# A recurrent-attention and mixture-of-experts layer: adaptation matmuls by sequence in column and row groups, router logits in four column groups turned by VectorE

## The chip, the core and the metric

The kernel runs on one core of one Trainium2 chip. The metric is the device time of one execution in microseconds; the time before is the median of three runs.

## The reference

32 sequences of 256 tokens with 128 channels, all in float32. The layer is a recurrent attention followed by a feed-forward layer with 16 experts, each with a residual and a layer norm:

```python
delta = shifted - h
x_lerp = h + delta * x_proj_mu
x0 = tanh(x_lerp @ xl_w1.T) @ xl_w2.T + xl_b2        # rank 32, then 5 * 32
x1 = tanh(x0).reshape(B, T, 5, 32)
mus = einsum('btnr,hnr->btnh', x1, x_out_w) + x_bias  # 5 mixing vectors per token
r, k, v, g, w = projections of (h + delta * mu_i)
o = scan over the tokens of S * w + k v, read with r, plus a bonus term
x = layernorm(h + (groupnorm(o) * gn_w + gn_b) * silu(g) @ o_w.T)
logits = x @ router_w + expert_bias                   # 16 experts
top 2 of the logits, softmax over the two
out = layernorm(x + shared_ffn(x) + weighted sum of the two experts' ffn(x))
```

The change touches the lines of `x0` and `x1` (called the adaptation here) and of `logits`.

## The kernel before

The work is in two stages. In the first, the 32 sequences are taken in 16 units of two sequences (512 tokens). In the second, the tokens, sorted by expert into DRAM, are taken in tiles of 256 rows through the experts; at the end the results are gathered and normed.

In the first stage each engine has a body written out by hand, with an offset for every step: `at(1, a_adapt0)` does step `a_adapt0` of unit i+1 in iteration i. So one iteration interleaves four units: the a-steps (mixing and projections) of one, the b-steps (attention in chunks of 32 tokens, in five levels) of the next older, the c-steps (norm, residual, router) of the one before that, and the f-steps (shared expert) of the oldest. Every engine runs its list in order; semaphores tie the lists together. A step waits with `done` for its inputs and with `before` for the last reader of what it overwrites.

TensorE's order in an iteration is: a_v, b_o, f_up 0, a_turn, c_place, level 0, f_up 1, a_adapt0, level 1, a_adapt1, f_up 2, level 2, mix w and r, f_up 3, decay_hid, level 3, w, r, c_attn, mix k and v, level 4, f_down, mix g, k, k_tok, c_turn, b_kv, c_logits, g. The steps that the change and the prediction touch:

- `a_adapt0` (TensorE, L331) multiplies the weights `xl_w1`, stored twice side by side (64 columns), with `x_lerp` of both sequences (512 columns) into bank P1, partitions 0 to 63. ScalarE's `a_adapt0` (L610) takes Tanh of it.
- `a_adapt1` (L337, L338) makes the 160 outputs in two matmuls of 32 rows: 128 outputs from partitions 0 to 31 into P0 and 32 outputs from partitions 32 to 63 into P1. ScalarE's `a_adapt1a` (L616) and `a_adapt1b` (L622) take Tanh with bias.
- `by_seq` (L309) is the form that the projections already have: one matmul per sequence, 64 outputs each, on output partitions 0 to 63 and 64 to 127. `mix` (L318) multiplies 32 rows of adapt1 by 128 outputs; mixes w and r, and k and v, stand in pairs, in different row groups and banks.
- `c_turn` (L466) transposes x; ScalarE copies it to x1T (L744). `c_logits` (TensorE, L472) uses each of the four 128-token tiles of x1T as weights and `router_w` (16 columns) as the moving side, so that the logits come out with tokens on partitions. VectorE's `c_logits` (L1089) adds the bias.
- VectorE's order behind that is: b_state (the scan, L1016), f_base (L1181), a_gate (L992), c_top (max, index, top_gap at L1103, chosen, either, seen up to L1114). TensorE's `c_place` (L478) waits for `seen`.
- ScalarE's order there is: x1T, b_kv (kv_sb, L704, which the scan waits for), a_k (L665, which TensorE's a_v waits for), k_near, gate, v, b_o.
- GpSimd's order is: rstd, step 4, chunk_decay, mixed V and G, scatter 0 (two indirect writes, L900, which wait for VectorE's slots), step 0 (L866, L868, L870), scatter 1, o_rstd, step 1, scatter 2, step 2, scatter 3, step 3. `b_step` i gives what level i+1 reads.

A float32 matmul shows as two records in the trace, each with its own weight load.

Of the kernel before, what the change touches and what calls it, by code (L numbers as in the profile page):

```python
# [17 lines left out]
UB = 2  # L18
# [22 lines left out]
COLS = (["x_mu", "xl_b2a", "xl_b2b"] + [f"x_bias{n}" for n in range(NMIX)] + ["w_b", "bonus", "gn_w", "gn_b", "tile_no", "tile_row", "par0", "par1"]  # L41
# [4 lines left out]
MATS = {"xl_w1": (C, 2 * RANK), "xl_w2": (2 * RANK, RANK * NMIX), "x_out_a": (128, C), "x_out_b": (RANK, C),  # L46
        "r_w": (C, HK), "k_w": (C, HK), "w_w1": (C, GATE), "w_w2": (UB * GATE, HK), "v_w": (C, HV), "g_w": (C, HV),
        "ident": (128, 128), "near": (128, L), "token_no": (128, TILES * TOPK),
        "o_w": (HV, C), "before": (128, 128), "ones": (128, 128), "router_w": (C, EXPERTS), "expert_bias": (128, EXPERTS),
# [9 lines left out]
def build(nc, hidden, mats_dram, cols_dram, masks_dram, w1_dram, w2_dram, b2_dram, out):  # L59
# [8 lines left out]
    with ctx:  # L68
# [34 lines left out]
        adapt0 = sb("adapt0", [2 * RANK, UT])  # L103
# [41 lines left out]
        logits = sb("logits", [128, TILES, EXPERTS])  # L145
# [48 lines left out]
        psP = [pb(f"psP{i}", [128, 512]) for i in range(2)]  # L194
# [4 lines left out]
        P0, P1 = psP[0][:, :], psP[1][:, :]  # L199
# [102 lines left out]
        def _(pe):  # L302
# [25 lines left out]
            def a_adapt0(u):  # L328
                before(pe, "gate", u)
                done(pe, "x_lerp", u)  # L330
                mm(P1[0:2 * RANK, :], mat("xl_w1"), flat(x_lerp), start=True, stop=True).then_inc(sem("adapt0_ps"))  # L331

            def a_adapt1(u):
                done(pe, "hT", u)
                done(pe, "adapt0", u)
                pe.nop(nofuse=True)
                mm(P0, mat("xl_w2")[0:RANK, 0:128], adapt0[0:RANK, :], start=True, stop=True)  # L337
                mm(P1[0:RANK, :], mat("xl_w2")[RANK:2 * RANK, 128:160], adapt0[RANK:2 * RANK, :], start=True, stop=True).then_inc(sem("adapt1_ps"))  # L338
# [130 lines left out]
            def c_logits(u):  # L469
                done(pe, "x1T", u)  # L470
                for j in range(TILES):
                    last = mm(O0[:, j * EXPERTS:(j + 1) * EXPERTS], x1T[u % 2][:, j * 128:(j + 1) * 128], mat("router_w"), start=True, stop=True)  # L472
                last.then_inc(sem("logits_ps"))
# [120 lines left out]
        def _(act):  # L594
# [11 lines left out]
            def a_adapt0(u):  # L606
# [3 lines left out]
                A(adapt0[:, :], P1[0:2 * RANK, :], ACT.Tanh).then_inc(sem("adapt0"))  # L610

            def a_adapt1a(u):
# [3 lines left out]
                A(adapt1a[:, :], P0, ACT.Tanh, bias=col("xl_b2a")).then_inc(sem("adapt1a"))  # L616

            def a_adapt1b(u):
# [3 lines left out]
                A(adapt1b[:, :], P1[0:RANK, :], ACT.Tanh, bias=col("xl_b2b", RANK)).then_inc(sem("adapt1b"))  # L622
# [133 lines left out]
            def body(at):  # L756
# [3 lines left out]
                at(-2, b_kv)  # L760
                at(-1, a_k)
# [190 lines left out]
        def _(dve):  # L952
# [131 lines left out]
            def c_logits(u):  # L1084
                if u == 0:
                    dve.wait_ge(sem("late_weights"), 16)
                done(dve, "logits_ps", u)
                dve.nop(nofuse=True)
                V.tensor_tensor(logits[:, :, :], O0[:, 0:TILES * EXPERTS].rearrange("p (n e) -> p n e", e=EXPERTS),  # L1089
                                mat("expert_bias").unsqueeze(1).broadcast_to([128, TILES, EXPERTS]), ALU.add).then_inc(sem("logits"))  # L1090

            def c_top(u):
# [3 lines left out]
                for j in range(TILES):  # L1096
                    last = V.max(top_val[:, j, :], logits[:, j, :])
# [3 lines left out]
                for j in range(TILES):  # L1101
                    last = V.max_index(top_idx[:, j, :], top_val[:, j, :], logits[:, j, :])
# [179 lines left out]
def pack(i):  # L1282
# [9 lines left out]
    put("xl_w2", np.tile(g("xl_w2").T, (2, 1)))  # L1292
# [11 lines left out]
    put("router_w", f("router_w"))  # L1304
    put("expert_bias", np.broadcast_to(f("expert_bias"), (128, EXPERTS)))
# [14 lines left out]
    for n in range(NMIX):  # L1320
        putc(f"x_bias{n}", g("x_bias")[n])
    putc("w_b", np.tile(g("w_b"), UB))
# [27 lines left out]
```

## Time and profile before

| | us |
|---|---|
| median of three runs (1012.99 to 1021.11) | 1017.16 |
| the profiled execution | 1020.37 |
| its span, first to last instruction | 1018.5 |
| TensorE (PE) busy | 847.5 (83%) |
| GpSimd (POOL) busy | 575.9 (57%) |
| VectorE (DVE) busy | 518.1 (51%) |
| ScalarE (ACT) busy | 488.0 (48%) |

The span has a start of some 110 us in which the pipeline fills, 13 like units up to about 555 us, a drain up to 660 us, the experts up to 950 us and the last norm. The mean granted TensorE clock is 0.921 of full speed (2.4 GHz); half of full speed is the other level, 1.2 GHz.

How to read it: PE is TensorE's matmuls and PEld its weight loads, which overlap them. Matmuls are pipelined, so the time of a record is longer than the distance to the next one; what a group costs is read from the distance between the starts of two groups, or from the chain that ended last, which counts each piece once. "x4" is the number of records in a group. The bracket behind a row says how long the engine was idle before it and who released it. Where two instructions of one engine overlap by a tenth of a microsecond, the second started before the first had written its last result.

### The profile page before, as it was taken

The numbers are of one execution on the slowest core, as the hardware profiler recorded it, in microseconds if no ns is written. First come the engines' busy times: TensorE is split into PE (matmuls) and PEld (weight loads), VectorE is DVE, ScalarE is ACT, GpSimd is POOL, SyncE is SP. The second block draws the span as 40 slices with busy tenths as digits, with TensorE's granted clock in tenths as the row PEclk, the third lists the DMA queues.
The fourth block names the chain that finished last, engine by engine and source line by source line (L and its number), as shares of the span: only waits on it lengthen the run. The fifth ranks groups of instructions, "written<-read, shape, count | busy, mean of one in ns | idle before, by whom it ended". The sixth has DMA issues, their size and how long they took to land.

```text
span 1018.5 us, 31274 instructions
## 1 busy us (share of the span) xinstructions
PE 847.5 (83%) x11556; PEld 597.0 (59%) x11557; DVE 518.1 (51%) x1478; ACT 488.0 (48%) x1121; POOL 575.9 (57%) x707
## 2 busy tenths in 40 slices
PE   4687999999989999999898856899999999999000
PEld 1233565456545554555455544799999999989000
DVE  2234576667676766676677443233333333322465
ACT  1233554555455545554555331466556666555244
POOL 2232556676667666766676747255555554555465
PEclk9976799999999999999999785899999999999655
DMA  4000111011101110111011331322222222221573
GB/s 136 21 2 6 34 50 49 27 51 55 49 25 55 52 52 24 53 54 52 24 50 33 96 103 51 100 74 64 74 66 71 62 62 71 59 61 36 164 224 107
DMA packets 74493, 63.67 MB, mean 63 GB/s; under 512 B 8178, under 2 KB 65912, under 8 KB 74256
## 3 DMA queue, kind: packets, MB, share of 16 engines
q1 hardware_dynamic: 56720, 40.86, 14.4%
q0 software_dynamic: 9216, 17.07, 5.1%
q10 hardware_dynamic: 8448, 4.20, 1.4%
q8 instruction: 79, 1.29, 0.5%
q14 instruction: 30, 0.25, 0.1%
HBM read 38.55 MB, written 25.63 MB: 63 GB/s over the span
## 4 chain that ended last, share of the span: by engine, by line
PE 69%; DVE 11%; issue 7%; ACT 5%; POOL 3%; DMA 2%; another core or an unknown queue 0%; DVEq 0%; SPq 0%; ACTq 0%; POOLq 0%
PE psO L573 14%; PE psB L562 13%; PE psB L408 7%; PE psO L507 6%; PE psP L318 6%; PE psO L501 4%; PE psP L309 3%; PE psP L337 2%; DVE top_gap L1103 2%; PE psB L427 2%; PE psP L331 2%; PE psP L553 2%; PE psP L338 2%; PE psO L460 2%; DVE mixed L983 1%
## 5 line engine op out<-in xcount | busy, mean ns | idle before, releaser
L934 POOL DMA_INDIRECT expert_results<-yw_all,rows x160 | 157.2, 983 | 158.4 <-ACT yw_all L799 129.5
L900 POOL DMA_INDIRECT dispatched_rows<-rows,slot x128 | 138.5, 1082 | 59.3 <-issue 29.3
L573 PEld LDWEIGHTS psO<-w_sb,hide 128*128 128x128 f32 x1280 | 154.8, 192 | 7.2 <-issue 3.5
L573 PE MATMUL psO<-w_sb,hide 128*128 x1280 | 156.5, 275 | 1.3 <-ACT hide L791 1.3
L791 ACT ACTIVATE hide<-psB,w_ring 128x256 f32<-128x256 f32 x320 | 125.1, 474 | 60.1 <-PE psB L562 56.5
L562 PE MATMUL psB<-x1T,w_ring 128*128 128x256 f32 x640 | 153.1, 382 | 0.3 <-DVE x1T L1224 0.2
L562 PEld LDWEIGHTS psB<-x1T,w_ring 128*128 128x128 f32 x640 | 116.3, 192 | 14.1 <-issue 1.2
L1237 DVE TENSOR_TENSOR kv_sb<-psO,b_sb 128x256 f32<-128x256 f32 x80 | 34.0, 425 | 176.7 <-PE psO L573 139.6
L799 ACT ACTIVATE yw_all<-kv_sb,rows 128x128 f32<-128x128 f32 x160 | 55.5, 394 | 81.4 <-issue 47.6
L983 DVE SCALAR_TENSOR_TENSOR mixed<-psP,cols,delta 128x512 f32<-128x512 f32 x80 | 58.0, 742 | 60.0 <-PE psP L309 31.6
L408 PEld LDWEIGHTS psB<-w_ring 32*32 32x32 f32 x4096 | 49.4, 108 | 65.8 <-issue 62.7
L501 PE MATMUL psO<-x1T,mats 128*128 128x512 f32 x128 | 78.4, 697 | 7.2 <-ACT w_sb L754 6.2
L1009 DVE COPY_PREDICATED pair<-masks,psB 128x512 f32<-128x512 uint32 x64 | 46.5, 726 | 60.8 <-PE psB L408 60.5
L408 PE MATMUL psB<-w_ring 32*32 32x64 f32 x4096 | 68.8, 239 | 9.3 <-issue 6.8
L754 ACT ACTIVATE w_sb<-psO,cols 128x512 f32<-128x512 f32 x64 | 43.3, 677 | 55.5 <-PE psO L501 49.2
L507 PE MATMUL psO<-mats,w_sb 128*128 128x128 f32 x512 | 65.1, 288 | 0.9 <-ACT w_sb L754 0.9
L507 PEld LDWEIGHTS psO<-mats,w_sb 128*128 128x128 f32 x512 | 62.1, 202 | 3.8 <-ACT w_sb L754 2.4
L885 POOL TENSOR_TENSOR o_rstd<-o_var,minus_half 128x16 f32<-128x16 f32 x16 | 50.9, 3182 | 19.0 <-DVE o_var L1027 16.2
L853 POOL TENSOR_TENSOR mixed<-mixed,hT 128x512 f32<-128x512 f32 x32 | 34.7, 1085 | 40.2 <-DVE mixed L983 40.2
L866 POOL TENSOR_TENSOR tot<-tot 128x64 f32<-128x64 f32 (+1 forms) x64 | 17.2, 269 | 70.6 <-PE psB L408 37.3
L733 ACT ACTIVATE rows<-z,z_shift,z_rstd 128x128 f32<-128x128 f32 x64 | 26.4, 482 | 59.8 <-DVE z_shift L1068 52.2
L1231 DVE COPY w_ring<-w_sb 128x516 f32 x80 | 34.4, 431 | 35.3 <-issue 35.3
(164 smaller groups left out, 1455.1 us busy)
## 6 DMA issues: line engine op xcount, KB each, us to landing
rows<-dispatched_rows SPq DMA_DIRECT2D x80, 132.0 KB
w_sb<-expert_results SPq DMA_DIRECT2D x16, 512.0 KB, 3.9
h_tok<-in_hidden SPq DMA_DIRECT2D x16, 256.0 KB, 4.7
h_res<-in_hidden SPq DMA_DIRECT2D x16, 256.0 KB, 3.2
out<-mixed ACTq DMA_DIRECT2D x16, 256.0 KB, 2.5
w_sb<-in_w SPq DMA_DIRECT2D x14, 256.0 KB, 4.8
expert_results<-yw_all,rows POOLq DMA_INDIRECT x160
dispatched_rows<-pad_rows SPq DMA_DIRECT2D x17, 132.0 KB, 3.7
```

The lines of the kernel that those rows point to most:

```text
L318: mm(ps, w, a, start=True, stop=True, **kw).then_inc(sem(f"mix_ps{n}"))
L408: last = mm(psL[32 * c4:32 * c4 + 32, g, c2 * 2 * L:(c2 + 1) * 2 * L].rearrange("p (a t) -> p a t", t=L), Ks[p, t], Rs[p, :, t], start=Tru ...
L501: mm(O1, mat("shared_w1")[:, c * 128:(c + 1) * 128], x1T[u % 2][:, :], start=True, stop=True).then_inc(sem(f"hid_ps{c}"))
L507: last = mm(O1[:, j * 128:(j + 1) * 128], hid[:, c, j * 128:(j + 1) * 128], mat("shared_w2")[:, c * 128:(c + 1) * 128], start=(c == 0), st ...
L562: last = mm(up_ps(p)[:, c // 2, (c % 2) * ST:(c % 2 + 1) * ST], w1b[i % W_RING][:, c * 128:(c + 1) * 128], xTe[p], start=True, stop=True)
L573: last = mm(psO[:, p, s * 128:(s + 1) * 128], hide[p][:, c, s * 128:(s + 1) * 128], w2_sb[:, bass.ds(e, 1), c, :].rearrange("p e c -> p (e ...
L791: last = A(hide[p][:, c, :], psB[:, 2 * p + c // 2, (c % 2) * ST:(c % 2 + 1) * ST], ACT.Relu, bias=w1b[i % W_RING][:, HIDDEN + c:HIDDEN + ...
L799: last = A(yw[i][:, s, :], ye[p][:, s, :], ACT.Copy, scale=row_in[i][:, s, AT_W:AT_W + 1])
L885: G.tensor_tensor(o_rstd[:, :], o_var[:, :], minus_half[:, :], ALU.pow).then_inc(sem("o_rstd"))
L900: G.indirect_dma_start(rows_dram[:, :], bass.IndirectOffsetOnAxis(slot[u % 2][:, j, k:k + 1], 0), rows[k][u % 2][:, j, :], None).then_inc( ...
L934: G.indirect_dma_start(back_dram[:, :], bass.IndirectOffsetOnAxis(row_in[i][:, s, AT_DEST:AT_DEST + 1].bitcast(u32), 0), yw[i][:, s, :], N ...
L983: V.scalar_tensor_tensor(mixed[MIX_BUF[n]][:, :, :], unflat((P0, P1)[MIX_BANK[n]]), col(f"x_bias{n}"), delta[:, :, :], ALU.add, ALU.mult). ...
```

## The change

The adaptation is done by sequence. `a_adapt0` uses `by_seq`: each sequence has its own 64 output partitions, and adapt0 becomes a tile of 128 partitions by 256 columns. `xl_w2` is stored four times, and `a_adapt1` has four matmuls of 256 columns: for the first 128 outputs of sequence 0 (rows 0 to 31) and sequence 1 (rows 64 to 95) into the first halves of P0 and P1, then for the last 32 outputs of both into the second halves. The two Tanh evictions read from both banks.

The router's weights are padded to 32 columns and become the stationary side; the tokens are the moving side, in four column groups. Column group q takes the q-th block of 32 tokens of each of the four tiles, 128 columns. The logits then have experts on partitions; ScalarE adds the bias while it copies them out of PSUM (a new step between b_kv and a_k), and VectorE transposes them in blocks of 32x32, which gives tokens on partitions again. VectorE no longer reads PSUM for them. The top-2 steps read the first 16 of 32 columns.

```diff
 MATS:
-"xl_w2": (2 * RANK, RANK * NMIX)
+"xl_w2": (UB * 2 * RANK, RANK * NMIX)
-"router_w": (C, EXPERTS), "expert_bias": (128, EXPERTS),
+"router_w": (C, L),
...
-        adapt0 = sb("adapt0", [2 * RANK, UT])
+        adapt0 = sb("adapt0", [UB * 2 * RANK, T])
...
-        logits = sb("logits", [128, TILES, EXPERTS])
+        logits_T = sb("logits_T", [128, TILES * L])
+        logits = sb("logits", [128, TILES, L])
...
-        psP = [pb(f"psP{i}", [128, 512]) for i in range(2)]
+        psP_both = pb("psP", [128, 2, 512])
+        psP = [psP_both[:, i, :] for i in range(2)]
...
             def a_adapt0(u):
                 before(pe, "gate", u)
                 done(pe, "x_lerp", u)
-                mm(P1[0:2 * RANK, :], mat("xl_w1"), flat(x_lerp), start=True, stop=True).then_inc(sem("adapt0_ps"))
+                by_seq(P1, mat("xl_w1"), x_lerp).then_inc(sem("adapt0_ps"))
...
-                mm(P0, mat("xl_w2")[0:RANK, 0:128], adapt0[0:RANK, :], start=True, stop=True)
-                mm(P1[0:RANK, :], mat("xl_w2")[RANK:2 * RANK, 128:160], adapt0[RANK:2 * RANK, :], start=True, stop=True).then_inc(sem("adapt1_ps"))
+                for b in range(UB):
+                    p = slice(64 * b, 64 * b + RANK)
+                    mm(psP[b][:, 0:T], mat("xl_w2")[p, 0:128], adapt0[p, :], start=True, stop=True)
+                for b in range(UB):
+                    p = slice(64 * b, 64 * b + RANK)
+                    last = mm(psP[b][0:RANK, T:2 * T], mat("xl_w2")[p, 128:160], adapt0[p, :], start=True, stop=True)
+                last.then_inc(sem("adapt1_ps"))
...
             def c_logits(u):
                 done(pe, "x1T", u)
-                for j in range(TILES):
-                    last = mm(O0[:, j * EXPERTS:(j + 1) * EXPERTS], x1T[u % 2][:, j * 128:(j + 1) * 128], mat("router_w"), start=True, stop=True)
+                pe.nop(nofuse=True)
+                x = x1T[u % 2][:, :].rearrange("p (n q t) -> p q n t", q=4, t=L)
+                for q in range(4):
+                    last = mm(O0[32 * q:32 * q + 32, 0:TILES * L].rearrange("p (n t) -> p n t", t=L), mat("router_w"), x[:, q, :, :],
+                              start=True, stop=True, tile_position=(0, 32 * q))
                 last.then_inc(sem("logits_ps"))
...
-                A(adapt0[:, :], P1[0:2 * RANK, :], ACT.Tanh).then_inc(sem("adapt0"))
+                A(adapt0[:, :], P1[:, 0:T], ACT.Tanh).then_inc(sem("adapt0"))
...
-                A(adapt1a[:, :], P0, ACT.Tanh, bias=col("xl_b2a")).then_inc(sem("adapt1a"))
+                A(unflat(adapt1a[:, :]), psP_both[:, :, 0:T], ACT.Tanh, bias=col("xl_b2a")).then_inc(sem("adapt1a"))
...
-                A(adapt1b[:, :], P1[0:RANK, :], ACT.Tanh, bias=col("xl_b2b", RANK)).then_inc(sem("adapt1b"))
+                A(unflat(adapt1b[:, :]), psP_both[0:RANK, :, T:2 * T], ACT.Tanh, bias=col("xl_b2b", RANK)).then_inc(sem("adapt1b"))
...
+            def c_logits(u):
+                done(act, "logits_ps", u)
+                before(act, "logits", u)
+                act.nop(nofuse=True)
+                A(logits_T[:, :], O0[:, 0:TILES * L], ACT.Identity, bias=col("router_b")).then_inc(sem("logits_T"))
...
                 at(-2, b_kv)
+                at(-3, c_logits)
                 at(-1, a_k)
...
             def c_logits(u):
-                if u == 0:
-                    dve.wait_ge(sem("late_weights"), 16)
-                done(dve, "logits_ps", u)
-                dve.nop(nofuse=True)
-                V.tensor_tensor(logits[:, :, :], O0[:, 0:TILES * EXPERTS].rearrange("p (n e) -> p n e", e=EXPERTS),
-                                mat("expert_bias").unsqueeze(1).broadcast_to([128, TILES, EXPERTS]), ALU.add).then_inc(sem("logits"))
+                done(dve, "logits_T", u)
+                V.transpose(logits[:, :, :].rearrange("p n e -> p (n e)"), logits_T[:, :]).then_inc(sem("logits"))
```

## Rows read from the trace of the kernel before

**Rows 1.** Windows: us, then busy us (instructions) PE, PEld, DVE, ACT, POOL, clock, DMA.
```profile
50.00:108.00 58.00, 47.88 (x779) 22.19 (x778) 24.97 (x43) 18.79 (x40) 21.47 (x34) 0.72 0.06 18
...
190.00:194.00 4.00, 4.00 (x69) 1.41 (x68) 0.93 (x4) 2.12 (x4) 2.81 (x4) 0.67 0.12 36
...
280.00:314.00 34.00, 31.19 (x593) 18.31 (x593) 23.66 (x66) 17.44 (x38) 23.22 (x29) 1.00 0.16 46
```

**Rows 2.** Chain that ended last, in order of time, 289 to 305: start, us.
```profile
289.83 1.00 PE psP L331 x2
...
291.64 1.09 PE psP L337 x2
...
292.74 0.97 PE psP L338 x2
...
294.76 0.62 PE psB L408 x36
...
301.91 0.58 PE psP L309 x4
...
303.58 1.10 PE psP L318 x4
```

**Rows 3.** Timeline, 290 to 300: start, us, engine, line, out<-in, idle before.
```profile
290.95 0.59 ACT L610 ACTIVATE adapt<-psP 64x512 f32<-64x512 f32 x1 [2.71 <-PE psP L331]
...
292.59 0.73 POOL L870 TENSOR_TENSOR w_ring<-w_ring,tot 128x256 f32<-128x256 f32 x1
...
298.17 1.01 POOL L900 DMA_INDIRECT dispatched_rows<-rows,slot  x1 [0.15 <-POOL w_ring L870]
...
298.60 0.69 DVE L988 TENSOR_TENSOR mixed<-mixed,hT 128x512 f32<-128x512 f32 x1
```

**Rows 4.** Timeline of PE in the first unit.
```profile
10.75 1.97 PE L331 MATMUL psP<-x_lerp,mats 128*64 128x512 f32 x2 [3.81 <-DVE x_lerp L972]
13.51 2.04 PE L337 MATMUL psP<-adapt,mats 32*128 32x512 f32 x2 [0.79 <-issue]
15.48 1.91 PE L338 MATMUL psP<-adapt,mats 32*32 32x512 f32 x2
...
22.61 1.12 PE L309 MATMUL psP<-mixed,mats 128*64 128x256 f32 x4 [1.70 <-DVE mixed L988]
```

**Rows 5.** Lines L628, L653, L1040: duration ns min/median/max.
```profile
L628 ACT ACTIVATE decay_hid<-psP x16: 383/383/384, 23.8 to 539.9; 128x256 f32<-128x256 f32 x16
...
L653 ACT ACTIVATE exp_w<-psP,cols x16: 473/473/475, 25.6 to 541.7; 128x256 f32<-128x256 f32 x16
...
L1040 DVE STREAM_TRANSPOSE w_sb<-w_sb x16: 683/691/711, 85.0 to 597.5; 128x512 f32<-128x512 f32 x16
```

**Rows 6.** Timeline, 312 to 322.
```profile
312.89 1.06 PE L472 MATMUL psO<-mats,x1T 128*128 128x16 f32 x8
...
313.52 0.68 ACT L704 ACTIVATE kv_sb<-psB 128x256 f32<-128x256 f32 x1
...
313.98 0.43 ACT L665 ACTIVATE w_ring<-psP 128x256 f32<-128x256 f32 x1
314.06 0.22 DVE L1089 TENSOR_TENSOR logits<-psO,mats 128x64 f32<-128x64 f32 x1 [0.23 <-PE psO L472]
314.32 1.22 DVE L1016 TENSOR_TENSOR_SCAN state<-chunk_decay,kv_sb 128x512 f32<-128x512 f32 x1
...
314.66 1.80 POOL L900 DMA_INDIRECT dispatched_rows<-rows,slot  x1 [1.76 <-DVE dest L1173]
...
317.74 1.71 DVE L1103 TENSOR_TENSOR top_gap<-top_val 128x4 f32<-128x4 f32 x1
...
318.58 0.84 POOL L870 TENSOR_TENSOR w_ring<-w_ring 128x256 f32<-128x256 f32 x1
...
321.16 0.43 PE L478 MATMUL psO<-either,mats 128*128 128x64 f32 x2 [0.63 <-DVE seen L1114]
```

**Rows 7.** Timeline, one scatter of a late unit.
```profile
582.51 1.10 POOL L900 DMA_INDIRECT dispatched_rows<-rows,slot  x1 [1.80 <-DVE dest L1173]
```

More of the change, by code:

```diff
@@ L39 @@
 MIX_BUF = {n: i % 2 for i, n in enumerate(MIX_ORDER)}
-COLS = (["x_mu", "xl_b2a", "xl_b2b"] + [f"x_bias{n}" for n in range(NMIX)] + ["w_b", "bonus", "gn_w", "gn_b", "tile_no", "tile_row", "par0", "par1"]
+COLS = (["x_mu", "router_b", "xl_b2a", "xl_b2b"] + [f"x_bias{n}" for n in range(NMIX)] + ["w_b", "bonus", "gn_w", "gn_b", "tile_no", "tile_row", "par0", "par1"]
         + [f"shared_b1_{c}" for c in range(HC)])
 COL = {n: i for i, n in enumerate(COLS)}
-MATS = {"xl_w1": (C, 2 * RANK), "xl_w2": (2 * RANK, RANK * NMIX), "x_out_a": (128, C), "x_out_b": (RANK, C),
+MATS = {"xl_w1": (C, 2 * RANK), "xl_w2": (UB * 2 * RANK, RANK * NMIX), "x_out_a": (128, C), "x_out_b": (RANK, C),
         "r_w": (C, HK), "k_w": (C, HK), "w_w1": (C, GATE), "w_w2": (UB * GATE, HK), "v_w": (C, HV), "g_w": (C, HV),
         "ident": (128, 128), "near": (128, L), "token_no": (128, TILES * TOPK),
-        "o_w": (HV, C), "before": (128, 128), "ones": (128, 128), "router_w": (C, EXPERTS), "expert_bias": (128, EXPERTS),
+        "o_w": (HV, C), "before": (128, 128), "ones": (128, 128), "router_w": (C, L),
         "expert_no": (128, EXPERTS), "region": (128, EXPERTS),
@@ L198, in build @@
         O0, O1 = psO[:, 0, :], psO[:, 1, :]
-        P0, P1 = psP[0][:, :], psP[1][:, :]
+        P0, P1 = psP
         flat = lambda t: t.rearrange("p a b -> p (a b)")
@@ L1096, in c_top @@
                 for j in range(TILES):
-                    last = V.max(top_val[:, j, :], logits[:, j, :])
+                    last = V.max(top_val[:, j, :], logits[:, j, 0:EXPERTS])
                 last.then_inc(sem("top_steps"))
@@ L1101, in c_top @@
                 for j in range(TILES):
-                    last = V.max_index(top_idx[:, j, :], top_val[:, j, :], logits[:, j, :])
+                    last = V.max_index(top_idx[:, j, :], top_val[:, j, :], logits[:, j, 0:EXPERTS])
                 V.tensor_tensor(top_gap[:, :], top_val[:, :, 1], top_val[:, :, 0], ALU.subtract).then_inc(sem("top_gap"))
@@ L1291, in pack @@
     put("xl_w1", np.tile(g("xl_w1").T, (1, 2)))
-    put("xl_w2", np.tile(g("xl_w2").T, (2, 1)))
+    put("xl_w2", np.tile(g("xl_w2").T, (UB * 2, 1)))
     put("x_out_a", g("x_out_w").T[:128])
@@ L1303, in pack @@
     put("ones", np.ones((128, 128), np.float32))
-    put("router_w", f("router_w"))
-    put("expert_bias", np.broadcast_to(f("expert_bias"), (128, EXPERTS)))
+    put("router_w", np.pad(f("router_w"), ((0, 0), (0, L - EXPERTS))))
     put("expert_no", np.broadcast_to(np.arange(EXPERTS, dtype=np.float32), (128, EXPERTS)))
@@ L1321, in pack @@
         putc(f"x_bias{n}", g("x_bias")[n])
+    putc("router_b", np.tile(np.pad(f("expert_bias"), (0, L - EXPERTS)), 4))
     putc("w_b", np.tile(g("w_b"), UB))
```

## The prediction

> **What bounds the kernel now.** I read the windows by stage first, then the chain that ended last in order of time, then the timeline of one unit. Of the 16 units (two sequences each) 13 run alike, with a new one begun every 34 us. In such a unit TensorE is busy 31.19 of 34 us at a granted clock of 1.00, which is 2.4 GHz [rows 1]. The chain shows that this is real: from the place matmuls (L478) to the KV matmuls it stays almost wholly on TensorE, and the three adaptation matmuls L331, L337 and L338 lie on it with 1.00, 1.10 (291.64 to 292.74) and 0.97 us [rows 2]. The rest of the unit is not TensorE's: from the eviction of kv_sb (ACT, L704) the chain goes to the scan (DVE, L1016), through VectorE's top-2 work to `seen`, and back to TensorE, which sat idle 0.63 us before L478 [rows 6]. So time off the adaptation counts in full, time off the logits matmuls counts only if the scan starts earlier, and anything put ahead of the scan costs.
>
> **adapt0.** One 128x64 matmul over 512 columns becomes two over 256 columns, on output partitions 0-63 and 64-127: exactly what `by_seq` (L309) does, four records in 0.58 us. Saved: 1.00 - 0.58 = 0.42 us. Tanh then reads 128x256 instead of 64x512: 0.59 us [rows 3] becomes 0.38 (L628, same form) [rows 5]. That matters only for whether adapt1 waits: the new adapt0 ends near 290.41, Tanh runs 290.53 to 290.91 (0.12 us for the hop, as from TensorE's end at 290.83 to Tanh at 290.95), and level 1 frees TensorE 0.42 us before 291.64, at 291.2. It doesn't wait, by about 0.2 us.
>
> **adapt1.** Before, L337 (32x128) and L338 (32x32) ran one after the other, 2.07 us together. After, there are two pairs of 256 columns; in each pair the two matmuls use row groups 0 and 64 and different banks. The nearest rows are L318, where two 32x128 matmuls over 512 columns in different row groups and banks take 1.10 us as a pair, and L309 with 0.58 for a pair of 256 columns [rows 2]. I take 0.63 for the first pair (128 weight columns) and 0.58 for the second: saved 2.07 - 1.21 = 0.86 us. Both ends: 2.07 - 2 x 0.55 (half of L318) = 0.97, and, should the pairs run singly, 2.07 - 4 x 0.58 = -0.25. I stay near L318, which is the same shape. The two Tanh that follow read as many columns as before, now from two banks: no cost.
>
> In a steady unit this is 1.28 us off the chain. What could take it back is what level 2 waits for: it starts at 294.76 and would start at 293.5; its latest input from GpSimd, L870, ends at 293.32 [rows 2, 3], and that itself follows level 1, so 0.2 us or more are left. Everything behind it to L427 is released by TensorE's own results and moves along. 13 x 1.28 = 16.6 us.
>
> The first unit runs at 1.2 GHz: L331 1.97 us, L337 and L338 together 3.88 (13.51 to 17.39), and the `by_seq` form 1.12 [rows 4]. Saved there: 0.85 + (3.88 - 2.24) + 0.21 of Tanh = 2.7 us. The second and third unit are partly at the low clock as well (0.72 on the mean from 50 to 108 us) [rows 1], but level 1 covers the Tanh and level 2 part of adapt1; I take 2.3 each. Together 7.3 us.
>
> **Router logits on TensorE.** Eight records with 128-column weight loads (0.91 us from L472 at 312.89 to the next matmul) become eight with 32-column loads in four column groups. Whatever they take up to 0.91 us, the result is there by about 314.0, and ScalarE is on kv_sb until then. What TensorE gains here is hidden: g follows earlier, but `a_v` waits for k_done. I cost it at nothing. If that cover went, it would be worth at most 0.6 us a unit.
>
> **Router logits on ScalarE and VectorE.** ScalarE gets one instruction more, a 128x128 eviction with bias from PSUM, between kv_sb and the copy of K (L665). From L610 and L628 a column costs 0.81 ns, so 128 columns take 0.28 us; the bias adds 0.09 (L653 against L628) [rows 3, 5]. It starts where L665 does now, 313.98, and ends at 314.35. VectorE's transposition can start 0.12 us later (the hop from kv_sb's end at 314.20 to the scan at 314.32), at 314.47. It replaces the addition L1089, and **the scan is behind it in VectorE's queue**. For its length, 512 columns took 0.69 (L1040) and so did the addition L988; with 0.22 for the 64 columns of L1089 that is 1.05 ns a column, so 0.29 us. Bounds: 0.17 (a quarter of L1040) and 0.35 (a half); for ScalarE 0.28 and 0.47. The scan starts at about 314.75 instead of 314.32 [rows 6]: 0.43 us late, between 0.23 and 0.6.
>
> Behind ScalarE's new wait stand the copy of K, k_near, the gate and v. K comes 0.3 us later and `a_v` waits for it, but `b_o`, the next on TensorE, waits for the scan's end, which is later still. Behind the scan stand base_out, the gate, the top-2 and `seen`, and TensorE waits for `seen`. Does GpSimd swallow it? top_gap (L1103), a 128x4 subtraction, took 1.71 us and ended with GpSimd's L870 at 319.4, so there is a stall that could absorb 0.43 us. But GpSimd's steps hang on the scan themselves: the scatter L900 began at 314.66, inside the scan, and ended 0.92 us after the scan's end (315.54) [rows 6]; free it takes 1.10 [rows 7]. So it asks for something that the scan holds 0.18 us after its start, at 314.84, and the scan will hold it from 314.75. Scatters, L866 to L870 and top_gap then move along with the scan, and the whole 0.43 us is paid: 13 x 0.43 = 5.6 us.
>
> A rule speaks for a higher price. The Trainium skill ("SBUF — State Buffer", section "SBUF: two separate sides") says that VectorE with two SBUF inputs and a GpSimd operation lock each other out, and that the one that starts first holds the port for its whole instruction. Top_gap against L870 agrees with it. Taken at its word, the scatter at 314.66 would now be first and hold the scan; see the third rival for what that gives.
>
> **Sum.** -16.6 - 7.3 + 5.6 = -18.3 us. The profiled execution took 1020.37 (span 1018.5), 3.2 more than the median; from it I would get 1002.1, from the median of 1017.16 it is 998.9. Forecast: 999.
>
> **Rivals.**
> 1. *The scatter gets ahead of the scan.* If the two hops cost 0.1 us more than I think, the scan starts behind 314.84, and the scatter ends at 315.8 instead of 316.46. GpSimd's steps end 0.7 us earlier, near 318.7, and top_gap with them. Then TensorE is the later one: 321.16 - 0.63 + 0.43 = 320.96, so L478 starts 0.20 us earlier than now, not 0.43 later [rows 6]. 13 x 0.63 = 8.2 us more: 991. My estimate misses this by only 0.1 us. Chance 0.17.
> 2. *The clock falls more often.* After the narrow matmuls of one unit the granted clock was 0.67 over 4 us, so 1.2 GHz for about 2.6 us of them [rows 1]. Shorter bursts with the same waits may bring that into every unit. Much of it falls in waits for VectorE; at 0.4 us a unit it costs 5 us: 1004. Chance 0.10.
> 3. *The scan is held by the scatter* until 315.76 and starts at 315.8: 1.5 us late, 13 x 1.5 = 19.5 instead of 5.6: 1013. Against it: L988, with two SBUF inputs, began 0.43 us into a scatter and took its ordinary 0.69 us [rows 3]. Chance 0.08.
> 4. *Row groups 0 and 64 don't overlap*, so the change doesn't do in adapt1 what it says: 13 x (0.42 - 0.25) = 2.2, early units some 1.5, less 5.6: 1019. L318 speaks against it. Chance 0.10.
> 5. *Slower: neither row nor column groups overlap in these places*, for instance because other tile shapes stand between them. adapt0 then costs 2 x 0.58 - 1.00 = 0.16 more and adapt1 0.25 more, 13 x 0.41 + 1.5 early = 6.8, plus 5.6: 1030. It turns to slower once the adaptation gains less than 0.43 us a unit. L309 and L318 both speak against it. Chance 0.04.
>
> **How the numbers follow.** Forecast 0.48 (its own range 994 to 1004), rivals 0.17, 0.10, 0.08, 0.10, 0.04, and 0.03 for something slower that I don't see. The range 987 to 1014 holds the forecast and the first three rivals, with some 4 us left for the spread of the runs at the lower end; above it are rivals 4 and 5 and the rest, 0.17. About 1% (10 us) is what a measurement of this kernel can tell from no change. Faster by over 1% (below 1007): 0.48 + 0.17 + 0.10 = 0.75. Within 1%: rivals 3 and 4, 0.18. Slower: rival 5 and the rest, 0.07.
>
> **What would show it.** Each step has its place in the profile after: adapt0 as four records in 0.6 us and adapt1 as eight in 1.2; level 2 about 1.3 us closer behind L478; the ScalarE eviction 0.37 and the transposition 0.29 us, with the scan right behind it; the first scatter still some 1.7 us long and top_gap some 1.7 (rival 1: scatter 1.1, top_gap 0.6 or less); the period 33.2 us instead of 34. The prediction is wrong if level 2 waits for GpSimd, if adapt1 shows four starts 0.5 us apart, or if the scan starts much more than 0.5 us after kv_sb.

## The result and the profile after

The change made the kernel slower: 1028.27 us (median of 6, 1023.91 to 1029.31) against 1017.7 for the kernel before beside it (6 runs), a ratio of 1.0082 with a 95% interval of 1.0053 to 1.0111. The forecast was 999, with a range of 987 to 1014. The profiled execution took 1023.91, its span was 1022.1 us and its mean clock 0.913. It was the shortest of the six, so the two profiles, spans of 1022.1 and 1018.5 us, show only 3.6 of the 10.6 us between the medians. Ratios and intervals are made from fast runs alone; of the runs below, three of the four of the kernel with the bad place (1068.87 to 1072.02, over 1.5% above its fastest, 1050.65) count as slow, and it has no ratio.

On the page of the profile after, PE is busy 16 us less than before (831.1 against 847.5). But the small matmuls of the levels, with the same count as before, now have 15.6 us of idle time behind which the profile shows no releaser ("issue"); before it was 6.8:

```profile
PE 831.1 (81%) x11652; PEld 589.7 (58%) x11653; DVE 517.9 (51%) x1478; ACT 487.4 (48%) x1137; POOL 579.0 (57%) x707
...
L415 PE MATMUL psB<-w_ring 32*32 32x64 f32 x4096 | 73.3, 243 | 16.8 <-issue 15.6
```

The same line of the page before:

```profile
L408 PE MATMUL psB<-w_ring 32*32 32x64 f32 x4096 | 68.8, 239 | 9.3 <-issue 6.8
```

The third scan starts at 132.64 instead of 143.53, so the early units gained 10.9 us; the forecast had 7.3. Behind the last steady scan they take 464.5 and 464.1 us. All of the loss lies in the 12 units between. Windows over them, first of before, then of after (us; busy us of PE, PEld, DVE, ACT, POOL; clock):

```profile
143.53:553.98 410.45, 377.42 (x7105) 221.69 (x7104) 284.20 (x793) 210.45 (x432) 278.52 (x348) 0.99 0.15 44
```
```profile
132.64:558.01 425.37, 372.86 (x7176) 219.90 (x7175) 284.19 (x793) 209.39 (x444) 282.85 (x349) 0.96 0.15 43
```

They grew by 14.9 us where the forecast had them shrink by 10. Each operation that the change touches is nevertheless nearly as short as forecast. adapt1 takes from 290.80 to 292.03, 1.23 us (forecast 1.21, before 2.07 [rows 2]), in the timeline of after:

```profile
290.80 0.75 PE L341 MATMUL psP<-adapt,mats 32*128 32x256 f32 x4
291.48 0.62 PE L344 MATMUL psP<-adapt,mats 32*32 32x256 f32 x4
292.03 1.12 PE L511 MATMUL psO<-x1T,mats 128*128 128x512 f32 x2
```

And the router's new way, in the same view, which answers to [rows 6]:

```profile
311.70 0.43 PE L481 MATMUL psO<-x1T,mats 128*32 128x128 f32 x8
...
312.06 1.13 PE L396 MATMUL psP<-mixed,mats 128*128 128x512 f32 x2
...
312.94 0.34 ACT L760 ACTIVATE logits_T<-psO,cols 128x128 f32<-128x128 f32 x1
...
313.31 0.31 DVE L1103 STREAM_TRANSPOSE logits<-logits_T 128x128 f32<-128x128 f32 x1 [0.52 <-ACT logits_T L760]
313.54 1.18 DVE L1033 TENSOR_TENSOR_SCAN state<-chunk_decay,kv_sb 128x512 f32<-128x512 f32 x1
313.62 2.01 POOL L917 DMA_INDIRECT dispatched_rows<-rows,slot  x1 [1.77 <-DVE dest L1186]
```

The logits matmuls take 0.36 us instead of 0.91, the eviction 0.34 (forecast 0.37), the transposition 0.31 (0.29), and the scatter still ends 0.9 us after the scan, as forecast.

One undisturbed unit, scan to scan, shows the failure in small: first of before, then of after.

```profile
348.46:382.54 34.08, 31.29 (x594) 18.39 (x592) 23.69 (x67) 17.53 (x37) 23.19 (x29) 1.00 0.16 45
```
```profile
347.78:381.88 34.10, 29.98 (x598) 18.09 (x598) 23.82 (x67) 17.50 (x38) 23.73 (x29) 1.00 0.16 46
```

TensorE is busy 1.31 us less, and the unit is as long as it was. The timeline of PE and POOL shows where it went. Before, level 2 (L408) was:

```profile
293.50 1.06 POOL L900 DMA_INDIRECT dispatched_rows<-rows,slot  x1 [0.17 <-POOL w_ring L870]
...
294.69 1.12 PE L408 MATMUL psB<-w_ring 32*32 32x64 f32 x50
294.86 0.96 POOL L900 DMA_INDIRECT dispatched_rows<-rows,slot  x1 [0.30 <-issue]
296.22 0.41 PE L408 MATMUL psB<-w_ring 32*32 32x64 f32 x14 [0.40 <-issue]
```

After (L415):

```profile
360.89 1.06 POOL L917 DMA_INDIRECT dispatched_rows<-rows,slot  x1 [0.17 <-POOL w_ring L887]
360.89 0.84 PE L415 MATMUL psB<-w_ring 32*32 32x64 f32 x45
362.15 0.32 PE L415 MATMUL psB<-w_ring 32*32 32x64 f32 x6 [0.42 <-issue]
362.25 0.96 POOL L917 DMA_INDIRECT dispatched_rows<-rows,slot  x1 [0.30 <-issue]
362.88 0.32 PE L415 MATMUL psB<-w_ring 32*32 32x64 f32 x5 [0.41 <-issue]
363.59 0.36 PE L415 MATMUL psB<-w_ring 32*32 32x64 f32 x8 [0.39 <-issue]
363.88 1.13 PE L320 MATMUL psP<-adapt1a,mats 32*128 32x512 f32 x4
```

Level 2 starts 1.3 us earlier against the scan, as forecast, and so comes to lie under both writes of scatter 2. After 45 records it proceeds by 5 to 8 records every 0.7 us, with gaps of 0.4, until the scatter has ended (363.21). Its last records start 0.38 us behind that end, and before they started 0.40 us behind it (296.22 against 295.82). The mix behind it (L320) starts 16.10 us after the scan, against 16.30 before. The gain is returned on the spot. In the kernel before, this wait already lay on the chain that ended last:

```profile
295.38 0.11 issue
295.50 0.32 PE psB L408 x5
295.82 0.40 issue
296.22 0.41 PE psB L408 x11
```

Six of the twelve units are 35.0 to 37.9 us long, and together they hold nearly the whole of the 14.9 us; the other six take 34.07 to 34.66. In five of the six long ones b_o (L454) stalls too; this is the unit from 275.99 (37.55 us):

```profile
278.33 0.82 PE L454 MATMUL psB<-state,w_ring 32*32 32x32 f32 x35
...
279.63 0.76 PE L454 MATMUL psB<-state,w_ring 32*32 32x32 f32 x51 [0.48 <-issue]
...
281.25 0.43 PE L454 MATMUL psB<-state,w_ring 32*32 32x32 f32 x26 [0.86 <-issue]
...
284.06 0.60 ACT L721 ACTIVATE o_sb<-psB 128x512 f32<-128x512 f32 x1 [4.33 <-remote]
...
284.91 0.61 PE L415 MATMUL psB<-R_near,K_near 32*32 32x64 f32 x39 [1.35 <-ACT o_sb L721]
```

The first gap, of 0.48 after 35 records, stands in every unit, before (0.46) as after. The second, 0.86 after 86, does not. In this unit ScalarE's copy of o also starts 2.4 us after b_o's end, and level 0 waits for it. That is dearer than the stall itself. In the units of this profile without a stall behind record 42 the copy starts 0.1 to 0.3 us after b_o's end; in the 18 profiles together it starts more than 0.5 us late only in units with such a stall, and then up to 2.8 us.

### The profile page after: what moved, and what is told of

Read it like the earlier page. It is cut to its first block, busy times and chain, and to the rows that moved or that the text cites. A ratio compares the mean times of both kernels' runs of the same rounds, so it can differ in the third digit from the quotient of the medians.

```text
span 1022.1 us, 31499 instructions
## 1 busy us (share of the span) xinstructions
PE 831.1 (81%) x11652; PEld 589.7 (58%) x11653; DVE 517.9 (51%) x1478; ACT 487.4 (48%) x1137; POOL 579.0 (57%) x707
## 3 DMA queue, kind: packets, MB, share of 16 engines
q8 instruction: 80, 1.31, 0.6%
## 4 chain that ended last, share of the span: by engine, by line
PE 70%; DVE 9%; issue 7%; ACT 6%; POOL 4%; another core or an unknown queue 2%; DMA 1%; ACTq 0%; DVEq 0%; SPq 0%; POOLq 0%
PE psO L583 14%; PE psB L572 14%; PE psB L415 7%; PE psP L320 6%; PE psO L511 5%; PE psO L517 5%; PE psP L311 4%; PE psB L434 2%; PE psO L467 2%; PE psP L563 2%; PE psB L454 1%; ACT mixed L836 1%; PE psP L341 1%; PE psP L367 1%
## 5 line engine op out<-in xcount | busy, mean ns | idle before, releaser
L511 PE MATMUL psO<-x1T,mats 128*128 128x512 f32 x128 | 87.0, 767 | 11.5 <-ACT w_sb L770 8.5
L415 PEld LDWEIGHTS psB<-w_ring 32*32 32x32 f32 x4096 | 51.7, 110 | 70.7 <-issue 67.9
L415 PE MATMUL psB<-w_ring 32*32 32x64 f32 x4096 | 73.3, 243 | 16.8 <-issue 15.6
L870 POOL TENSOR_TENSOR mixed<-mixed,hT 128x512 f32<-128x512 f32 x32 | 34.7, 1085 | 36.8 <-DVE mixed L1000 36.8
```

Of the source, the lines that this page charges most:

```text
L415: last = mm(psL[32 * c4:32 * c4 + 32, g, c2 * 2 * L:(c2 + 1) * 2 * L].rearrange("p (a t) -> p a t", t=L), Ks[p, t], Rs[p, :, t], start=Tru ...
L511: mm(O1, mat("shared_w1")[:, c * 128:(c + 1) * 128], x1T[u % 2][:, :], start=True, stop=True).then_inc(sem(f"hid_ps{c}"))
```

## The experiments

The theories were these. *Supply*: TensorE's instructions arrive too slowly where many short matmuls stand together, either because GpSimd's scatters run beside them or because of where the blocks lie in which they are fetched (the page shows 80 packets and 1.31 MB in an instruction queue, so 16 KB each; I took a block to be 256 instructions). *Logits*: the scan's delay is dearer than I thought. *Clock*: the changed rhythm lowers the clock. Each group of runs had its own runs of the kernel before, with which the ratios are made (medians 1005.02, 1022.85, 1019.48 and 1021.79 us).

### First group: the halves, a shift, the scatters moved

The adaptation alone (all of the diff's lines on adapt0, adapt1, psP and `xl_w2`):

> Only the adaptation by sequence; the logits as in the kernel before. Theory A (TensorE's instructions come late in level 2 whenever the adaptation is shorter): the 1.3 us saved per unit come back as idle time ended by issue in level 2, so the time is near the kernel before, 1008 to 1020 (the early units keep some 7 us). Rival B (the loss is the scan behind the new logits steps, 0.4 us a unit): without them the adaptation's gain shows in full, about 993.

978.11 us (977.53 to 986.29), ratio 0.9729 (0.9653 to 0.9805), with units of 31.9 to 32.9 us. The logits alone (the rest of the diff):

> Only the router logits in column groups with the transposition; the adaptation as before. Rival B: 13 units x 0.4 us later scan, about 1023, and no further idle time in level 2. Theory A: the same 0.4 us a unit on the scan, but one issue gap of 0.4 us in level 2 as before, and in b_o further issue gaps only where a block of instructions ends in it; 1020 to 1030.

1012.44 us, ratio 1.0046 (0.9998 to 1.0093): no gain, and perhaps a loss, with b_o stalls of 1.1 to 1.7 us in six units. Then the whole change with 60 instructions put in at the start of TensorE's stream:

```diff
             pe.wait_ge(sem("weights"), 32)
+            for _ in range(15):
+                mm(psP[0][0:32, 0:8], mat("ident")[0:32, 0:32], mat("ident")[0:32, 0:8], start=True, stop=True)
```

> The changed kernel with 15 small matmuls (60 instructions, under 1 us, before the first input is there) at TensorE's start, nothing else. Theory C (in some units b_o is held where TensorE's instruction stream passes the end of a block of 256): the units with a long gap in b_o move by one, since every unit moves the place by some 30 records and the shift moves it back by 30; time within 5 us of the changed kernel. Rival: the long gaps come from transfers of that moment (loads of h and weights, scatters), then they stay in the same units (third, sixth, seventh, eleventh, twelfth).

989.71 us, ratio 0.9822 (0.9758 to 0.9886): the time did not stay within 5 us of the changed kernel. The b_o stalls did move by one unit, as the place in the stream would have it: in after they stand in units 3, 7, 11 and 12, here in 4, 8, 12 and 13. And the whole change with two scatters behind the GpSimd steps that level 3 and 4 need:

```diff
-                at(-1, c_scatter, 2)
                 at(2, b_step, 2)
-                at(-1, c_scatter, 3)
+                at(-1, c_scatter, 2)
                 at(2, b_step, 3)
+                at(-1, c_scatter, 3)
```

> The changed kernel with GpSimd's scatters 2 and 3 behind its steps 2 and 3 instead of ahead of them, so that none is issued while TensorE is in level 2. Theory A, with the scatters as the cause of the late instructions: the three gaps of 0.4 us in level 2 go, level 3 may get some, 0.5 to 1.2 us a unit, 1012 to 1022. Rival (instructions come at a fixed rate whatever GpSimd does): the gaps in level 2 stay and the time is that of the changed kernel, 1028.

987.38 us, ratio 0.981 (0.9741 to 0.9878). Read alone, this says that the shift cured the kernel. The traces say something else: in all four the gaps in level 2 and the 0.46 us gap in b_o are missing in nearly every unit, in those without a shift as well; and with no gaps to cure, the moved scatters gained nothing over the shift. Level 2 of the adaptation alone ran beside the same scatter without a halt:

```profile
305.96 1.04 PE L414 MATMUL psB<-w_ring 32*32 32x64 f32 x64
305.99 1.06 POOL L906 DMA_INDIRECT dispatched_rows<-rows,slot  x1 [0.17 <-POOL w_ring L876]
306.93 1.13 PE L319 MATMUL psP<-adapt1a,mats 32*128 32x512 f32 x4
```

The kernel before was faster here as well (1005.02, against 1019 to 1023 in all later groups). So the unshifted kernels had to be run again.

### Second group: controls

> The changed kernel once more, nothing altered, as the control for the shifted one and the one with the scatters moved. If the place of TensorE's instruction stream decides (theory A), it is 0.5 to 1.1% slower than the kernel before again, with two kinds of stalls in its trace: three gaps of about 0.41 us within the 64 small matmuls of level 2 in every unit, and gaps of 0.7 to 1.4 us within b_o in some units. If the stalls belong to the chip or to where the program was loaded on it (theory B), it is 1.5 to 3% faster here, with a steady period of about 32.1 us and no gap in level 2, like its shifted copy.

1034.29 us, ratio 1.0095 (1.0069 to 1.0122): the loss is real, and the gaps are back.

> The kernel before once more, nothing altered, for its trace on this chip. Theory A (place of the stream): steady periods of 34.0 to 34.4 us again, with one gap of 0.40 us in level 2 after 50 matmuls. Theory B (chip or loading): no gap of 0.40 in level 2 and periods of about 33.6 us (34.08 less the 0.40); its time within 1% of its own earlier median on this chip.

1020.65 us, ratio 0.9976 (0.9949 to 1.0004): periods of 34.1 us and the gap of 0.42 in level 2 in every unit.

> The kernel before with 60 more instructions (15 tiny fp32 matmuls into a scratch bank) at the start of TensorE's stream, nothing else. Theory A: its time moves by 0.5 to 3% either way against the kernel before, and the gaps within b_o turn up in other units. Theory B: within 0.3% of the kernel before, since the sum of its stalls is the same wherever the blocks of instructions lie.

1026.82 us, ratio 1.0054 (1.0024 to 1.0084): small, but three b_o stalls instead of one in the units 2 to 15. It is 0.6% over the unchanged copy e6, at the low end of what the place of the blocks was expected to do.

> The changed kernel with 120 more instructions (30 tiny fp32 matmuls) at the start of TensorE's stream. Theory A: its time differs from the unshifted one of the same chip by over 1%, as the copy with 60 would have to. Theory B: within 0.3% of the unshifted one run beside it.

1037.42 us, ratio 1.0123 (1.0081 to 1.0166). That is 0.3% over the unshifted copy e5, not the 1% or more that was expected of the place of the blocks. The shift is no cure. What sets the first group apart isn't the kernel; nor is it the chip, since the last group below ran on the same one and has the gaps. That stays open.

The controls also price the clock. The unit from 355.43 of the unchanged copy has the same gaps as the unit of after shown above, at a clock of 0.91 instead of 1.00, and takes 1.9 us longer:

```profile
355.43:391.44 36.01, 32.71 (x598) 18.79 (x598) 23.66 (x67) 17.51 (x38) 23.84 (x29) 0.91 0.15 43
```

### Third group: the place of the blocks, the scatters again

```diff
             def c_place(u):
+                pad(O0, 14)
+                nc.tensor.transpose(O0[0:32, 300:332], mat("ident")[0:32, 0:32], mat("ident")[0:32, 0:32])
                 done(pe, "seen", u)
```

> The changed kernel with TensorE's instruction stream padded: tiny matmuls of 32x8 into a part of the bank that nothing reads, 23 before the first input and, in each unit, 14 and a turn of 32x32 ahead of the wait for seen, so that the stream advances by 1279 instructions a unit (5 times 256 less 1) instead of 1221. Theory A (b_o stalls where the stream passes instruction 194 modulo 256 and the block behind it is not there yet): this point now lies after 21 to 27 of b_o's 112 matmul records in every unit from the second on, where no profile has shown a stall; no gap over 0.3 us follows there in any unit (the one after 34 to 36 records, of 0.46 to 0.50 us, may stay), no unit of 37 us is left, and the kernel is 10 us or more faster than its twin with the bad place. Theory B (the stalls in b_o come from transfers or scatters that run beside it): some four to six units have them still, at other records, and the twins agree within 0.5%.

> The twin of the one before: the same 14 tiny matmuls and the turn in each unit, but none before the first input, so that instruction 194 modulo 256 lies after 66 to 73 of b_o's 112 records in every unit from the second on. Theory A: a gap of 0.4 to 1.7 us at just that record in 14 of 16 units, periods 1 to 3.5 us longer than with the good place, in sum 15 to 45 us slower than its twin. Theory B: within 0.5% of it.

1023.39 us (1017.56 to 1027.74) with the good place; 1050.65, 1068.87, 1070.01 and 1072.02 with the bad one. The two kernels differ by 92 instructions ahead of the first input. The comparison to rest on is with the one run of 1050.65: 27 us, and still 23 above the longest run with the good place. How much of the rest, up to 49 us, belongs to the place is not shown. The profile is of the run of 1072.02. b_o with the good place, then with the bad:

```profile
275.27 0.82 PE L462 MATMUL psB<-state,w_ring 32*32 32x32 f32 x35
...
276.56 1.00 PE L462 MATMUL psB<-state,w_ring 32*32 32x32 f32 x77 [0.47 <-issue]
```
```profile
289.87 0.82 PE L461 MATMUL psB<-state,w_ring 32*32 32x32 f32 x35
...
291.19 0.58 PE L461 MATMUL psB<-state,w_ring 32*32 32x32 f32 x34 [0.50 <-issue]
...
292.19 0.65 PE L461 MATMUL psB<-state,w_ring 32*32 32x32 f32 x43 [0.42 <-issue]
```

The stall behind records 67 to 73 stands in all units from 3 to 15 of the bad one, and in none of the units 2 to 15 of the good one. The units 4 to 14 take 38.2 to 40.5 us against 34.2 to 36.3. A stall of 0.4 us is the least of it: in the units 4 to 15 ScalarE's copy of o starts 2.4 to 2.8 us after b_o's end, with the good place 0.12; f_up (L520) waits up to 1.55 us for ScalarE; and the clock over the twelve units is 0.83 instead of 0.94:

```profile
134.24:554.73 420.49, 381.59 (x7524) 224.45 (x7523) 282.71 (x792) 209.61 (x444) 282.26 (x348) 0.94 0.15 43
```
```profile
132.33:601.27 468.94, 421.24 (x7524) 237.31 (x7523) 284.47 (x792) 209.47 (x444) 278.47 (x348) 0.83 0.13 39
```

But the good place doesn't win either: 1.003 (0.9998 to 1.0062). Its level 2 gaps are all there.

> Only the adaptation by sequence, with the logits as before, padded in the same way with the good place (records 21 to 34). If the logits' new form is what makes b_o's block come late (it did in 6 of 6 places between records 56 and 111, the adaptation alone in 3 of 7), this is as fast as or faster than the padded full change; against the kernel before it is 1.5 to 3.5% faster. If the adaptation's many short matmuls are the burden, it loses against the kernel before on a chip with gaps in level 2.

1018.77 us, ratio 0.997 (0.9946 to 0.9994): the lower end of what was expected is missed; the level 2 gaps eat this version's gain too.

> The changed kernel with the scatters of a tile behind the products of steps 2 and 3 on GpSimd rather than ahead of them, for its trace on this chip. If the scatters that run under level 2 hold TensorE's supply of instructions up (three gaps of about 0.41 us), the gaps go or move to level 3, where the scatters now run, and step 2 starts right behind the matmuls. If the gaps belong to level 2's own 64 matmuls, they stay.

998.55 us, ratio 0.9806 (0.9738 to 0.9873), in a group whose other kernels have the gaps. This is the cure. Between scan 3 and scan 15 no scatter touches level 2 any more. Level 2 runs through, and the mix starts 14.11 us after the scan instead of 16.10:

```profile
313.42 0.85 PE L415 MATMUL psB<-w_ring 32*32 32x64 f32 x64
314.21 1.13 PE L320 MATMUL psP<-adapt1a,mats 32*128 32x512 f32 x4
...
315.84 1.06 POOL L917 DMA_INDIRECT dispatched_rows<-rows,slot  x1 [0.18 <-POOL w_ring L887]
```

The scatter's first write now runs beside a matmul of 512 columns, which needs few instructions, and a wait; the second reaches into level 3 and leaves a gap of 0.2 us there. The window over the twelve units, with the same instructions as after:

```profile
134.71:528.40 393.69, 353.20 (x7176) 213.68 (x7175) 283.74 (x793) 209.68 (x444) 283.75 (x348) 1.00 0.16 46
```

The clock stays at 1.00, and PE's busy time falls from 372.86 to 353.20 us for the same instructions. Not all of that is the clock: in a clean unit, at 1.00 in both, PE is busy 29.98 us in after and 29.50 here.

### Fourth group: what belongs to the change

> The kernel before with the same reordering on GpSimd (each of the scatters 2 and 3 behind the product of its step), nothing else. If the reordering alone made the 1.9%, this is as fast as the changed kernel with it: ratio 0.98. If it only gives back what the change had lost to the gaps, the kernel before gains its own one gap of 0.42 us and little more: periods of 33.6 us, ratio 0.990 to 0.998.

1021.09 us, ratio 0.9983 (0.996 to 1.0005). The reordering gives the kernel before nothing that can be measured; its clean units go from 34.1 to 33.66 us, and a clock of 0.98 takes part of that back:

```profile
143.96:553.15 409.19, 377.11 (x7105) 220.85 (x7104) 284.76 (x793) 210.18 (x432) 277.93 (x348) 0.98 0.16 44
```

> The adaptation by sequence alone, logits and scatters as before. If the gaps in level 2 eat the adaptation's gain on a chip that has them, it shows three gaps of about 0.42 us in a unit, periods near 34 us, and a ratio of 0.99 to 1.00; if the chip has none, periods of 32.1 us and a ratio of 0.973 as before. If it was the logits that cost the time, it keeps 0.97 to 0.98 on either.

1022.86 us, ratio 1.0003 (0.9976 to 1.0031). In most units three gaps, 1.2 to 1.3 us together, and a clock of 0.93 over the twelve: the adaptation's gain is gone without any help from the logits.

> The adaptation by sequence alone with the scatters moved. By the forecast's terms the adaptation is worth 1.3 us a unit of PE time and the logits' new form costs 0.4 us of waiting: so 0.3 to 0.8% faster than the whole change with the scatters moved, ratio 0.973 to 0.978, with no unit over 34.5 us. If the logits' new form does help (its matmuls are shorter), it is slower than that: 0.981 or more.

994.98 us (994.31 to 997.85), ratio 0.9747 (0.9719 to 0.9776), clean units of 32.4 us. This is the best version, with the old logits.

> The same, padded by 14 tiny matmuls and a turn a unit and 23 at the start, so that instruction 194 modulo 256 lies in records 21 to 34 of b_o. If the blocks still cost something, the two or three stalls of 0.5 to 1.4 us in b_o go, and it gains 0 to 3 us; if the padding costs more than them (it lies in the wait for seen, 0.7 us in the unpadded kernel), it is 0 to 6 us slower.

999.65 us, ratio 0.9796 (0.9767 to 0.9825): no stall in b_o is left in units 2 to 15, but the pad costs 0.2 us in each unit and 4.7 us in all. Once the scatters are moved, the place of the blocks isn't worth paying for.

## Why the prediction was wrong

**adapt0 and adapt1: right.** 1.31 us less PE time in a unit against 1.28. With the scatters moved it also arrives in the period: 33.66 us for the kernel before (e13), 32.41 for the adaptation alone (e15), 1.25 us.

**The early units: right in kind, the size not settled.** 10.9 us gained up to the third scan instead of 7.3 (the terms from [rows 4] and the low clock of [rows 1]). But between the unchanged copies (e6 and e5) it is 139.32 against 136.85, 2.5 us. One profile of each kernel doesn't settle the size.

**"Everything behind it to L427 is released by TensorE's own results and moves along": the step that failed.** I had asked whether level 2 would wait for an *input* from GpSimd, and found 0.2 us of room. That was right: no semaphore that the profile shows holds it. But its 64 records get through at only 5 to 8 in 0.7 us while scatter 2 runs, against all 64 in 0.85 us without it. So the last of them start some 0.4 us after the scatter has ended, before as after, though the level starts 1.3 us earlier. The scatter hangs on GpSimd's chain and the scan; its second write ends 15.57 us after the scan's start before and 15.43 after. Taking 1.3 us of TensorE work out ahead of the level could thus not shorten the unit. That what runs short is the supply of instructions (the 64 records are 128 of them) is argued from the idle time without a releaser. These gaps are not the block ends: they stand behind much the same records of every unit, at a different place modulo 256 each time. e14 (the adaptation alone, 1.0003) and e12 (0.9806) against e13 (0.9983) show it from both sides. The trace of before had the hint: level 2 broke off after 50 records for 0.40 us with "issue" behind it (shown above), and the chain of [rows 2] lists only 36 records of L408 at 294.76, where I had left out the 0.40 us of "issue" behind them. I read the idle times of PE for what released them, and passed over those that nothing released.

**The clock: rival 2, with too small a price.** It was given 0.4 us a unit and 5 us. In the twelve units the mean fell from 0.99 to 0.96, and to 0.93 in the unchanged copy (e5); a mean of 0.96 is 8% of 425 us, 34 us, at the lower level. One unit at 0.91 costs 1.9 us. With the scatters moved the clock is 1.00 (e12). Level 2's gaps are not its only cause: in e3 and e4, without them but with b_o stalls of over 1 us, it was 0.97 and 0.96. What each gap does to the clock wasn't measured apart.

**b_o: not in the prediction at all.** The change makes a unit 1221 instructions long instead of 1208, and so alters in which units instruction 194 modulo 256 falls into b_o's records 56 to 111. That is chance, nearly: six candidates among units 2 to 15 before, seven after. What isn't chance is how many of them stall. Over the profiles, kernels with the new logits stalled at 52 of 59 such places (units 2 to 15), those with the old at 12 of 45. At a stall the block was late, as its packets show; why it is late more often with the new logits is only argued: the new logits matmuls take 0.36 us instead of 0.91 for the same number of instructions, shortly ahead of b_o, so the next block has less time to come. Five of the six long units in the profile after have such a stall. This is probably what made the kernel slower instead of leaving it as it was: without these stalls, and with a pad that costs time itself, the change stood at 1.003 (e9), with them at 1.0082 and 1.0095 (e5).

**The logits: right in kind, smaller in the clean unit, dearer in the end.** The scan was to be 0.43 us late. Counted from the start of the KV matmuls it is 0.27 late (2.70 us, 310.84 to 313.54, against 2.43, 311.89 to 314.32), within the stated bounds: the transposition began 0.03 us after the eviction's end, not 0.12. With the scatters moved, the kernels with and without them differ by 0.2 us in their clean units (32.6 and 32.4), 2.4 us over twelve, and by 0.6% (6 us) in all (e12 and e15, each by its ratio to the kernel before). Another 3 us lie in the second unit (33.5 against 30.2 us), where b_o stalls for 1.99 us with the new logits and not with the old. Alone they cost 0.5% (interval from 0 to 0.9%). The scatter didn't hold the scan (rival 3). In the units 4 to 14 it didn't get ahead of it either (rival 1), though it began only 0.07 to 0.08 us behind the scan's start in ten of these eleven. In units 3 and 15 it did get ahead, by 0.09 us; this is unit 15:

```profile
557.92 1.10 POOL L917 DMA_INDIRECT dispatched_rows<-rows,slot  x1 [1.76 <-DVE dest L1186]
558.01 1.18 DVE L1033 TENSOR_TENSOR_SCAN state<-chunk_decay,kv_sb 128x512 f32<-128x512 f32 x1
```

Here neither holds the other. The Trainium skill's rule on the shared port ("SBUF — State Buffer", section "SBUF: two separate sides") agrees with the units in which the scan was first and the scatter ended 0.91 us behind it; in unit 15 the scatter was first and the scan took its ordinary 1.18 us beside it, so there the rule, taken at its word, is no guide. Nor does top_gap bear it out as I had written: it began 0.01 us ahead of GpSimd's L866 and still ended only with L870. That shows top_gap held up beside GpSimd's steps, but not that the first one keeps the port:

```profile
317.75 0.41 POOL L866 TENSOR_TENSOR tot<-w_ring 128x128 f32<-128x128 f32 x1
```

**Row and column groups (rivals 4 and 5)** overlap as the change says: adapt1's four matmuls of 256 columns take 1.23 us, and the logits' four 0.36.

**What stays open.** Why the first group of runs had no gaps: level 2 lay under the same scatter there, so the scatter is needed for the gaps where they occur, and isn't enough by itself. Why ScalarE's copy of o starts up to 2.8 us after b_o's end in units with a stall: the profile names no engine of this core. And whether the scatter slows TensorE through its own transfers or through GpSimd; only that moving it away helps is shown.

The Trainium skill ("Runtime: NRT & Kernel Launch", section "Instruction fetch mechanics") says that instructions are fetched in blocks of 256 and that crossing from one to the next is mostly hidden. The blocks agree with the seventy gaps at one place modulo 256. "Mostly hidden" doesn't hold in b_o, whose 112 records, 224 instructions, take 1.3 to 1.5 us where nothing halts them: the stalls there measured 0.29 to 1.99 us.

## What to carry to other kernels

- Where an engine's idle time has no releaser ("issue") and lies inside a dense run of small instructions, treat it as a limit of its own: ask what runs beside it at that moment, and whether work saved ahead of it would only make it start earlier into the same limit.
- Where such gaps show, try GpSimd's indirect writes beside long matmuls instead of many short ones. Here this turned +0.9% into -1.9%, and with the old logits -2.5%, by moving two lines.
- Before a shift or a small edit is believed to have helped, run the unedited kernel beside it: 60 more instructions seemed to bring 2.7%, and it was the group of runs.

## What the hardware showed that I had not expected

- b_o's stalls stand at one place of the instruction stream modulo 256 in 70 of 79 cases, and padding by 92 instructions at the start moved the time by 27 us or more (1023 against 1051, and 1069 to 1072 in three further runs) once the unit's length was a near multiple of 256.
- In the shifted copy of the first group, where b_o stalled, the instruction packet nearest ahead of the stall began 0.5 to 1.5 us before TensorE halted, and TensorE went on 1.3 to 1.5 us after that packet's end; over all the profiles it was 1.2 to 1.6 us.
- ScalarE's copy of o came up to 2.8 us late behind a stall of b_o of only 0.4 us.
- While an indirect write of GpSimd ran, TensorE got 5 to 8 small matmul records in about 0.7 us; without one it takes 64 records in 0.85 us.
